# A third batch of the second FFN prepared in the tail of attention, the quotient on Pool moved behind the first search, and the last batch's projection moved inside step 2

## What is computed

```python
x = x + 0.5 * ffn(layernorm(x))     # first FFN
x = x + attention(layernorm(x))     # 16 heads of 16
x = x + 0.5 * ffn(layernorm(x))     # second FFN, same weights as the first
```

## Time and profile before

| | us |
|---|---|
| median of 3 runs | 3456.27 (3455.72 to 3456.39) |
| the profiled execution | 3455.7 |
| its span, first to last instruction | 3453.9 |
| PE, DVE, ACT, POOL busy in the span | 3259.7, 3006.9, 2705.0, 1069.3 |
| routing stage of the second FFN begins | 3134.4 |
| searches of batches 0, 1, 2, 3 begin | 3146.96, 3164.50, 3176.91, 3187.21 |
| slot stage of the second FFN begins | about 3328 |

### The profile page before, as it was taken

One profiled execution on the slowest core, in us unless ns is written; L12 is line 12 of the kernel. 1 busy time (PEld: TensorE's weight loads), 2 busy tenths in 40 slices (PEclk: granted clock), 3 DMA queues, 4 the chain that ended last, 5 costly groups with the idle time before them and its releaser, 6 DMA issues. The chain is left out here.

```text
span 3453.9 us, 61039 instructions
## 1 busy us (share of the span) xinstructions
PE 3259.7 (94%) x22602; PEld 1162.5 (34%) x22602; DVE 3006.9 (87%) x4477; ACT 2705.0 (78%) x5326; POOL 1069.3 (31%) x1020
## 2 busy tenths in 40 slices
PE   6997799999999999999999999999999999998997
PEld 4654222323222323232323232323232323224654
DVE  6865889999999999999999999999999998995865
ACT  5841488888888888888888888888888888886840
POOL 2440133333333333333232323232323232122410
PEclk8998799999999999999999999999999999999998
DMA  4337121313131313131313121312131222213336
GB/s 133 98 138 285 49 69 33 81 33 81 33 81 33 81 33 82 33 81 35 79 36 78 39 76 40 77 39 76 39 76 43 72 43 61 57 41 96 98 124 268
DMA packets 184779, 263.32 MB, mean 76 GB/s; under 512 B 96340, under 2 KB 137108, under 8 KB 170148
## 3 DMA queue, kind: packets, MB, share of 16 engines
q1 hardware_dynamic: 177700, 256.28, 26.7%
q10 hardware_dynamic: 6784, 3.15, 0.4%
HBM read 121.91 MB, written 51.38 MB: 50 GB/s over the span
## 5 line engine op out<-in xcount | busy, mean ns | idle before, releaser
L1674 DVE TENSOR_REDUCE attn_part_max<-attn_ps 128x2 f32<-128x1024 f32 x2048 | 2442.4, 1220 | 207.5 <-PE attn_ps L1803 172.9
L1921 ACT ACTIVATE attn_probs<-attn_ps 128x512 f32<-128x512 f32 x4096 | 2161.1, 598 | 365.5 <-PE attn_ps L1816 365.4
L1816 PE MATMUL attn_ps<-attn_q_rows,attn_k_rows 50*128 50x512 f16 x4096 | 1258.8, 384 | 43.0 <-ACT attn_probs L1921 25.2
L1803 PE MATMUL attn_ps<-attn_k_rows,attn_q_rows 48*128 48x512 f16 x4096 | 1129.3, 386 | 19.9 <-DVE attn_part_max L1674 19.1
L1830 PE MATMUL attn_ps<-attn_probs,attn_v_ones 128*32 128x512 f32 x8192 | 1092.7, 605 | 0.7 <-ACT attn_probs L1921 0.7
L1816 PEld LDWEIGHTS attn_ps<-attn_q_rows,attn_k_rows 50*128 50x128 f16 x4096 | 308.0, 94 | 1327.1 <-ACT attn_probs L1921 1212.5
L1566 POOL CAST attn_max_parts<-attn_max_whole 16x128 f16<-16x128 f32 x128 | 36.0, 281 | 1161.3 <-ACT attn_max_whole L1869 1161.2
L1803 PEld LDWEIGHTS attn_ps<-attn_k_rows,attn_q_rows 48*128 48x128 f16 x4096 | 224.0, 94 | 160.9 <-DVE attn_part_max L1674 140.4
L1830 PEld LDWEIGHTS attn_ps<-attn_probs,attn_v_ones 128*32 128x32 f32 x8192 | 161.2, 108 | 246.5 <-issue 153.2
L1765 PE MATMUL attn_ps<-attn_shared,attn_w_qk 128*128 128x256 f16 x1536 | 211.8, 275 | 19.8 <-PEq L26 19.8
L1611 POOL TENSOR_TENSOR attn_alpha_t<-attn_alpha_t 128x256 f32<-128x256 f32 x120 | 88.0, 733 | 294.3 <-ACT attn_alpha_t L1898 258.4
(11 more groups left out here) (200 smaller groups left out, 2548.9 us busy)
## 6 DMA issues: line engine op xcount, KB each, us to landing
attn_q_rows<-attn_alpha_t SPq DMA_DIRECT2D x384, 64.0 KB, 2.2
attn_k_rows<-attn_alpha_t SPq DMA_DIRECT2D x384, 64.0 KB, 2.3
ffn_x_back<-in_L_attn_x SPq DMA_DIRECT2D x16, 1024.0 KB, 13.1
after_first_ffn<-ffn_x_back SPq DMA_DIRECT2D x16, 1024.0 KB, 13.0
attn_slot_out<-attn_alpha_t SPq DMA_DIRECT2D x256, 64.0 KB, 2.4
attn_alpha_t<-inverse_denominators SPq DMA_DIRECT2D x32, 512.0 KB
attn_alpha_t<-after_first_ffn SPq DMA_DIRECT2D x16, 1024.0 KB, 9.9
after_attention<-attn_alpha_t SPq DMA_DIRECT2D x16, 1024.0 KB, 4.3
```

The costliest lines, as they stand in the source:

```text
L1674: dve.tensor_reduce(part_max[:, G % 2, j, :, t, half], pair, AX.X, ALU.max).then_inc(dve_emptied, 1)
L1803: last = pe.matmul(ps[:, bank + e, :], q_rows[rows_e, G % NG, j, t * P:(t + 1) * P], k_rows[rows_e, G % NG, j, half * HALF:(half + 1) * HA ...
L1816: pe.matmul(ps[:, bank, :], k_rows[rows_e, G % NG, h // 2, kt * P:(kt + 1) * P], q_rows[rows_e, G % NG, h // 2, half * HALF:(half + 1) * H ...
L1921: act.activation(probs[:, quad % NQ, h, :], bank_of(s, b0), ACT.Exp, scale=1.0 / (SCALE * SCALE)).then_inc(act_emptied, 1)
```

## The change

- `AHEAD` goes from 2 to 3. A new buffer `third` holds the third early batch; `x_ring` shrinks by one slot, and the slot stage's `pre` moves into `third`. `load_ahead` loads three batches on one semaphore, and the statistics wait for all three. VectorE prepares batch 2 in attention's tail: its statistics behind the normalising of batch 0, its normalising at the end. In the second FFN `statistics(2)`, `rsqrt(2)` and `normalise(2)` on both engines are gone, and batch 3 is the first that SyncE loads there.
- `divide_last` on GpSimd moves into step 0, behind `less_largest(0)` and `rsqrt(3)`, ahead of `scale(0)`.
- `project_last(0, 1)` moves into step 2 between `turn_rows(3, (0, 1))` and `logits(2)`; `project_last(2, 3)` stays behind `turn_rows(3, (2, 3))` in step 2. `add_last` moves to the head of VectorE's steps 2 and 3, ahead of the searches.
- Semaphores are merged: `last_ctx_step` for three, `x_in_place` by slot with counts that go on. The first FFN has the same loops as before; only one of its slots lies elsewhere.

```diff
-        AHEAD, TURNED = (2, 1) if ending else (0, 0)
+        AHEAD, TURNED = (3, 1) if ending else (0, 0)
...
-            x_ring = sb("x_ring", [P, R - 2, TT, D + 1], F32, own)
-            x_slots = c.x_first + [x_ring[:, r] for r in range(R - 2)]
+            x_ring = sb("x_ring", [P, R - 3, TT, D + 1], F32, own)
+            x_slots = c.x_first + [x_ring[:, r] for r in range(R - 3)]
...
                 for b in range(AHEAD, 3):
                     rsqrt(b)
-                if ending:
-                    divide_last()
                 for n in range(B):
                     less_largest(n)
                     if n + 3 < B:
                         rsqrt(n + 3)
+                    if ending and n == 0:
+                        divide_last()
                     scale(n)
...
                 for n in range(STEPS):
+                    if ending and 2 <= n < 4:
+                        add_last(2 * n - 4, 2 * n - 3)
                     if n < B:
                         find_top(n)
-                    if n + 2 < B:
+                    if AHEAD <= n + 2 < B:
                         normalise(n + 2)
                     if n + 3 < B:
                         statistics(n + 3)
                     if n < B:
                         weigh(n)
-                    if ending and 1 <= n < 3:
-                        add_last(2 * n - 2, 2 * n - 1)
...
-                pe.wait_ge(ones_set, 3)
+                pe.wait_ge(ones_set, 4)
...
                     if n + 1 < B:
                         turn_rows(n + 1, (0, 1))
+                    if ending and n == 2:
+                        project_last(0, 1)
                     if n < B:
                         logits(n)
                     if n + 1 < B:
                         turn_rows(n + 1, (2, 3))
-                    if ending and 1 <= n < 3:
-                        project_last(2 * n - 2, 2 * n - 1)
+                    if ending and n == 2:
+                        project_last(2, 3)
...
-                    if n % 2 == 0 and n + 2 < B:
+                    if n % 2 == 0 and AHEAD <= n + 2 < B:
                         normalise(n + 2)
...
-                sp.wait_ge(stored, 16 * 2)
-                for i in range(2):
-                    sp.dma_start(c.x_first[i][:, :, 0:D], rows(x_out, i, i)).then_inc(c.ahead_loaded[i], 16)
+                sp.wait_ge(stored, 16 * 3)
+                for i in range(3):
+                    sp.dma_start(c.x_first[i][:, :, 0:D], rows(x_out, i, i)).then_inc(c.ahead_loaded, 16)
...
-                dve.wait_ge(c.ahead_loaded[i], 16)
+                dve.wait_ge(c.ahead_loaded, 16 * 3)
...
             ahead_statistics(0)
             ahead_statistics(1)
             ahead_normalise(0)
+            ahead_statistics(2)
             ahead_normalise(1)
+            ahead_normalise(2)
```

More of the change, by code:

```diff
@@ L51, in build_shared @@
     shared = sb("shared", [P, 3, TT * (D + 1)])
-    c.x_first = [shared[:, i].rearrange("p (t d) -> p t d", t=TT) for i in range(2)]
+    c.third = sb("third", [P, TT * (D + 1)])
+    c.x_first = [rows.rearrange("p (t d) -> p t d", t=TT) for rows in (shared[:, 0], shared[:, 1], c.third[:, :])]
     flat = [shared[:, i, 0:TT * D] for i in range(3)]
@@ L65, in build_shared @@
     c.b_v_wide_ready, c.fold_ready, c.b_o_ready = sem("b_v_wide_ready"), sem("fold_ready"), sem("b_o_ready")
-    c.ahead_stats, c.ahead_mean_var = sb("ahead_stats", [P, 2, TT, 6]), sb("ahead_mean_var", [P, 2, TT, 2])
-    c.ahead_var_eps, c.ahead_rstd = sb("ahead_var_eps", [P, 2, TT]), sb("ahead_rstd", [P, 2, TT])
-    c.ahead_loaded, c.ahead_step = [sem(f"ahead_loaded{i}") for i in range(2)], sem("ahead_step")
+    c.ahead_stats, c.ahead_mean_var = sb("ahead_stats", [P, 3, TT, 6]), sb("ahead_mean_var", [P, 3, TT, 2])
+    c.ahead_var_eps, c.ahead_rstd = sb("ahead_var_eps", [P, 3, TT]), sb("ahead_rstd", [P, 3, TT])
+    c.ahead_loaded, c.ahead_step = sem("ahead_loaded"), sem("ahead_step")
     c.ahead_var, c.ahead_root, c.ahead_normal = sem("ahead_var"), sem("ahead_root"), sem("ahead_normal")
@@ L597, in project_last @@
                 def project_last(*numbers):
-                    pe.wait_ge(c.last_ctx, 1)
+                    pe.wait_ge(c.last_ctx_step, 3)
                     for n in numbers:
@@ L716, in build_ffn @@
             gates, new_t, mix_z = c.shared
-            pre = sb("pre", [P, 2, KT, HALF], F32, own)
+            pre = c.third[:, 0:2 * KT * HALF].rearrange("p (h k n) -> p h k n", h=2, k=KT)
             cand = sb("cand", [P, 2, KT, HALF], F32, own)
@@ L754, in build_ffn @@
             b_out_loaded = sem("b_out_loaded")
-            x_in_place = [sem(f"x_back_in{p}") for p in range(PAIRS)]
+            x_in_place = [sem(f"x_back_in{p}") for p in range(RP)]
             stored = [sem(f"stored{p}") for p in range(PAIRS)]
@@ L777, in load @@
                     for e in range(2):
-                        sp.dma_start(x_back[:, p % RP, e], rows(x_in, 2 * p + e)).then_inc(x_in_place[p], 16)
+                        sp.dma_start(x_back[:, p % RP, e], rows(x_in, 2 * p + e)).then_inc(x_in_place[p % RP], 16)
                 def store(p):
@@ L1051, in add_back @@
                         if i == 0:
-                            dve.wait_ge(x_in_place[p], 32)
+                            dve.wait_ge(x_in_place[p % RP], 32 * (p // RP + 1))
                         dve.wait_ge(mixed, n + 1)
```

12 lines of the change are left out of this document (6 added, 6 removed).

## The result

| | before | after |
|---|---|---|
| median, us (lowest to highest) | 3458.08 (3455.47 to 3461.86), 13 runs | 3445.67 (3440.61 to 3450.8), 13 runs |
| ratio after / before, 95% interval | | 0.9965, 0.9957 to 0.9973 |
| the profiled execution, its span | 3455.7, 3453.9 | 3448.82, 3447.0 |
| first DMA of the stage | 3134.43 | 3134.26 |
| searches 0, 1, 2, 3 | 3146.96, 3164.50, 3176.91, 3187.21 | 3142.96, 3151.49, 3167.66, 3177.96 |

The change makes the kernel 12 us faster (9 to 15 by the interval). Two more comparisons with runs of their own gave 0.9966 (0.9954 to 0.9979) and 0.9968 (0.9957 to 0.998).

The account below looks back on a forecast made before the run. Waits ahead of search 0 and in steps 0 and 1 of the second FFN lose about 9 us. Search 3 gains 10.9 us, less 0.1 elsewhere: 10.8 off the median 3456.27 gives 3445.5 us, range 3443.0 to 3448.8.

Parts of the forecast that it names:

- Search 0 and step 0: Second FFN: search 0 at 3143.3, search 1 at 3151.8; step 0 8.5 us instead of 17.54.
- both causes named for step 0: Step 0: batch 2's load and preparation (VectorE waits 5.34 us), and the 5.76 us quotient ahead of `less_largest(0)` on GpSimd.
- The stage's start and attention's tail: Batch 2's preparation fits attention's tail on VectorE with 6.5 us of cover; the stage still begins at 3134.4.
- C: Rival: batch 2's preparation sticks out of attention's tail and the gain doesn't arrive; 3455 us, chance 0.05.
- D: Rival: the third early load delays the row maxima on SyncE's queue, TensorE stands in attention; 3465 us, chance 0.04.
- B: Rival: a late landing replaces the removed wait, batch 4 costing 5 us or the inverse 3.8; 3449.5 us, chance 0.08.
- Search 2: End of step 1: search 2 at 3165.7, 13.9 us after search 1 instead of 12.41; wrong if after 3167.
- the bound of `normalise(3)`: VectorE, step 1: at most two waits of 3.40 against 1.38 us, ending by 3159.3 instead of 3157.3; adds 0.3 us.
- The projection's cover: TensorE: first projection, 2.78 us, fits in the wait for batch 2's gelu with 2.6 us left, costing nothing.
- Rival A: TensorE's clock falls to half in step 2, costing 1.4 to 1.9 us on search 3; 3447.2 us, chance 0.15.
- Search 3 and the sum: Search 3 at 3176.0 instead of 3187.21: 11.2 us earlier, 10.9 against the same arithmetic over the old order.
- The shared port: VectorE and GpSimd lock their SBUF port pair, the loser blocks; quotient across `normalise(3)` makes the sum 0.3 us worse.

Follow-up runs that it names:

- e1: Third early batch only, with quotient, projection and additions in their old places, against the kernel before: 3458.34 us, ratio 1.0002.
- e2: Moves of quotient, projection and additions only, with two early batches instead of three, against the kernel before: 3457.46 us, ratio 1.0.
- e9: Changed kernel with VectorE's four tiles of `normalise(3)` done by ScalarE: 3447.45 us, ratio 0.9976 to the kernel before.
- e7: Changed kernel with SyncE spreading the last batch's inverse denominators ahead of batch 3's load: 3455.95 us in one run.
- e8: As e7, and on GpSimd the quotient also ahead of `rsqrt(3)`: 3446.21 us, ratio 0.9965 to the kernel before.
- e5: Changed kernel with the quotient's product, cast and subtraction cut to 16 of 1024 columns, the other columns left out: 3442.99 us in one run.
- e10: As e9, and GpSimd's quotient moved behind `less_largest(1)` instead of ahead of `scale(0)`: 3450.44 us in one run.
- e4: Changed kernel with only `project_last` and `add_last` put back in their old places: 3451.22 us in one run.
- e6: Changed kernel with the quotient's cast and subtraction each cut into two halves of 512 columns: 3448.91 us.

## Why the prediction was right, and where it was not

The forecast was 3445.5 us in 3443.0 to 3448.8; the median is 3445.67. That the two agree within 0.2 us is luck: the forecast took 10.8 us off a median of 3456.27, while the runs beside the changed kernel gave 3458.08 before and 12.4 us less after. Point by point:

- **Search 0 and step 0**: right. Search 0 came at 3142.96 (said 3143.3), `hidden(1)` took 3.70 us (said 3.60) behind 0.74 of idle (said 0.7), search 1 was at 3151.49 (said 3151.8). e1 and e2 show that both causes named for step 0 were real, and that neither can be had alone; the prediction's parts don't say this.
- **The stage's start and attention's tail**: right. The stage begins at 3134.26, and VectorE does the third batch in the gap it had:

```profile
3115.01 2.67 DVE L1730 TENSOR_SCALAR attn_third<-attn_third,attn_ahead_mean_var,attn_ahead_rstd 128x256 f32<-128x256 f32 x8
3117.60 0.68 DVE L1743 COPY attn_shared<-attn_ps 128x512 f32<-128x512 f32 x1
3119.74 0.69 DVE L1743 COPY attn_shared<-attn_ps 128x512 f32<-128x512 f32 x1 [1.46 <-PE attn_ps L1852]
...
3127.00 0.69 DVE L1743 COPY attn_shared<-attn_ps 128x512 f32<-128x512 f32 x1 [1.74 <-PE attn_ps L1852]
```

  One copy comes late, and the last waits for TensorE as before. Rivals C and D did not occur. Nor did B in its full size: no load ended a wait of VectorE from search 0 on, and only in the profile beside e9 did GpSimd wait for the inverse, 0.55 us. The runs e7 and e8, where batch 3's load lands late, show what such a landing costs: 5.8 us of step 0.
- **Search 2**: wrong. It came at 3167.66, past the 3167 named as the mark; step 1 took 16.17 us, not 13.9. The step that failed is the bound of `normalise(3)`, "say two such waits, ending by 3159.3". Each of the four instructions waited, for the cast, the subtraction, `scale(0)` and `less_largest(1)`, and it ended at 3160.4. The row with 3.40 us was read as one blocked instruction, which was true there, but only because three of the four had started before the product did (3151.16 in the earlier trace rows). The fourth, from a narrow window of the kernel before, met it alone:

```profile
3151.36 2.44 DVE L480 TENSOR_SCALAR ffn_x_ring<-ffn_x_ring,ffn_mean_var,ffn_rstd 128x256 f32<-128x256 f32 x1
```

  The rule that it stood for is one turn each. With it, 1.04 + 2.12 + 1.04 + 1.06 us and the handovers make about 5.5 us.
- **The projection's cover**: lost, by that and by the clock. Of the 2.3 us, 0.45 are GpSimd's chain: `rsqrt(3)` took 2.14 us, not 1.64, because VectorE's `weigh(0)` now stood beside it, which the row of 1.64 us in the earlier trace rows did not have. The projection began 9.94 us behind search 1 instead of 6.3, which used the 2.6 us of cover and about 0.3 more. The other 1.65 are its own length at half clock. e9 gives the cover back; e5 shows the step with the clock up as well, but also without the quotient's length.
- **Rival A**: it had 0.15, and it came true, in another place than said: ahead of search 2, on the first projection, and not behind it on the second. Of the profiles with the moved quotient and the third batch, all nine in which TensorE waited for 1.6 us or more between the searches 1 and 2 show a half-clock stretch that begins between 3157 and 3166; the tenth, e5, waited 0.74 us at most and shows none. This is what followed what in ten profiles; no run changed the wait alone. On this point the Trainium skill, page "TensorE: Matmul & The Clock Gate", section "HAM oscillation", was the better guide: in its example the gap between two bursts is paid every time. The trace agrees in step 1, with 4.45, 4.46 and 4.33 us for a projection of 2.78 in the changed kernel, e10 and e4, but not at the stage's start: `hidden(0)` waits 1.62 us in all ten, and a half-clock stretch lies over it in five of them.
- **Search 3 and the sum**: 9.1, 10.5 and 11.0 us won from the stage's start in the three profiles, against 10.9. The forecast is close for a reason that it did not have: step 1 lost 2.3 us more, and in two of the three profiles `hidden(0)` ran at full clock and gave back 1.45 us or more that the profile of before had lost at the earlier trace rows and the sum had carried along.
- **The rest of the 12 us** isn't shown by any single pair of profiles. The piece behind search 15 varies by 4.4 us with the same instructions, and attention's end by 6.5; how the means of these pieces stand in the two kernels was not measured.
- **The shared port.** The Trainium skill, page "SBUF — State Buffer", section "SBUF: two separate sides", has the pair as a lock held for a whole instruction, the other engine blocked. The prediction weighed it at 0.3 us. The trace agrees with the lock: `normalise(3)` took 4.1 us more than alone. What the turns cost on the path is read from e9, where they are gone and the quotient stays: `logits(2)` 2.1 us earlier behind search 1, search 2 0.9 to 1.4 us earlier, and search 3 0.5 us or nothing, as the clock took the rest. The 5.5 us of e5 are the price of the quotient in this place, turns included.

No version tried here beats the changed kernel. e5 marks what is left for one that gets the quotient out of step 1: some 5 us at search 3.

## What to carry to other kernels

Before you put work of GpSimd beside work of VectorE, write both queues side by side and pair them instruction by instruction: a VectorE step of short instructions of the kind of `normalise` pays one whole GpSimd instruction for each of its own. In e10 the statistics beside the same quotient paid nothing (2.70 us, as alone), so measure the kind first. Give a wait of TensorE its price at half clock, not only its length: three edits that shortened the path here but left TensorE a wait of 1.6 to 2.9 us (e6, e9, e10) gave all or most of the gain back. And where two waits run side by side, test the parts of a change together, since each alone may show nothing.

## What the runs showed that was not expected

- The instructions of `normalise` and those of GpSimd take strict turns, with GpSimd nearly undisturbed: `normalise(3)` 5.52, 5.53, 5.17 and 5.05 us beside whole instructions, 3.80 beside halves, 1.50 and 1.51 beside the end of one only; GpSimd's whole subtraction 2.12 or 2.13 in every case.
- The other way round, GpSimd's root takes 2.13 us instead of 1.64 wherever VectorE's product of `weigh` has begun just ahead of it, 47 times of 47; this stands in nearly every step and is no part of the change.
- A store of 32 KB behind a load of 1 MB in the same queue landed after 5.1 to 5.7 us in eleven profiles, ahead of it after 1.9 in the two others.
- Two of three profiles of the same kernel had `hidden(0)` at 3.70 us and one at 5.15: in that one a half-clock stretch lay over it (3134.2 to 3137.5), in the two others the clock was full from 3085 to 3157; single runs of the changed kernel reach from 3440.6 to 3451.8 us.
